# Transposing the normed rows with DMAs instead of TensorE

## The reference, cut to what matters

```python
x = _layernorm(x + _L0_attn_ref(x, ...), axis=-1)

def _L0_ffn_ref(x, wq_gate, s_gate, wq_up, s_up, wq_down, s_down):      # DIM 512, HID 1408
    gate = silu(qlinear(x, wq_gate, s_gate))      # (wq - 128) * scale, summed over DIM
    up = qlinear(x, wq_up, s_up)
    return qlinear(gate * up, wq_down, s_down)

x = _layernorm(x + _L0_ffn_ref(x, ...), axis=-1)
```

## Time and profile before

| | before |
|---|---|
| median of 3 runs | 1080.04 us |
| the profiled execution's own time | 1076.37 us |
| its span, first to last instruction | 1074.6 us |
| PE busy | 1030.4 us (96%) |
| VectorE (DVE) busy | 780.8 us (73%) |
| GpSimd (POOL) busy | 640.9 us (60%) |
| ScalarE (ACT) busy | 465.0 us (43%) |
| mean busy share of the DMA engines, SP's queue | 26.8% |

### The profile page before, as it was taken

One profiled execution on the slowest core, in us unless ns is written; L12 is line 12 of the kernel. 1 busy time (PEld: TensorE's weight loads), 2 busy tenths in 40 slices (PEclk: granted clock), 3 DMA queues, 4 the chain that ended last, 5 costly groups with the idle time before them and its releaser, 6 DMA issues.

```text
span 1074.6 us, 18114 instructions
## 1 busy us (share of the span) xinstructions
PE 1030.4 (96%) x6426; PEld 837.3 (78%) x6426; DVE 780.8 (73%) x1426; ACT 465.0 (43%) x994; POOL 640.9 (60%) x683
## 2 busy tenths in 40 slices
PE   7996889999999999999999999999999999989996
PEld 5576678888888888888888888887878888877774
DVE  6576766787878777786877778786777878676554
ACT  4655443534444344544445343444445344424242
POOL 4456866476756747565764756575674667575210
PEclk9898989999999999999999999999999999999998
DMA  7554302231132222322122222312121211322232
GB/s 231 171 157 152 114 31 59 89 89 50 46 95 77 79 59 80 92 66 70 49 80 88 79 60 87 92 40 89 50 79 50 88 51 42 96 60 79 89 99 79
DMA packets 51640, 89.55 MB, mean 83 GB/s; under 512 B 6298, under 2 KB 11034, under 8 KB 51550
## 3 DMA queue, kind: packets, MB, share of 16 engines
q1 hardware_dynamic: 50786, 88.12, 26.8%
q10 hardware_dynamic: 764, 0.27, 0.1%
HBM read 77.09 MB, written 11.27 MB: 82 GB/s over the span
## 4 chain that ended last, share of the span: by engine, by line
PE 73%; DVE 9%; POOL 7%; issue 7%; ACT 3%; DMA 1%; ACTq 0%; POOLq 0%; DVEq 0%
PE gate_up L997 11%; PE gate_up L998 11%; PE bank L862 9%; PE bank L864 9%; PE bank L863 9%; PE down L1008 6%; PE down L1009 6%; PE bank L958 3%; POOL acc L628 2%; DVE tmp L756 1%; PE bank L980 1%; POOL acc L635 1%; PE spectrum L863 1%; PE spectrum L864 1%; PE spectrum L862 1%
## 5 line engine op out<-in xcount | busy, mean ns | idle before, releaser
L593 ACT ACTIVATE hid<-gate_up,gate_scale 128x256 f32<-128x256 f32 x176 | 83.0, 472 | 208.6 <-PE gate_up L998 204.6
L756 DVE TENSOR_TENSOR tmp<-spectrum,filt 128x512 f32<-128x512 f32 x250 | 169.2, 680 | 0.0
L997 PE MATMUL gate_up<-x2T_hi,wg_sb 128*128 128x256 f16 x704 | 165.8, 276 | 0.0
L634 POOL TENSOR_TENSOR acc<-acc,tmp 128x256 f32<-128x256 f32 x156 | 121.0, 776 | 73.9 <-DVE tmp L756 63.9
L998 PE MATMUL gate_up<-x2T_lo,wg_sb 128*128 128x256 f16 x704 | 163.8, 273 | 0.0
L998 PE MATMUL gate_up<-x2T_lo,wu_sb 128*128 128x256 f16 x704 | 163.3, 273 | 0.0
L997 PE MATMUL gate_up<-x2T_hi,wu_sb 128*128 128x256 f16 x704 | 163.2, 273 | 0.0
L1008 PE MATMUL down<-wd_sb,hid_hi 128*128 128x512 f32 x352 | 148.2, 421 | 5.7 <-DVE tmp L799 3.1
L862 PE MATMUL bank<-xT_hi,win_hi 128*128 128x512 f32 x360 | 150.3, 417 | 2.0 <-POOL win_lo L611 1.7
L864 PE MATMUL bank<-xT_hi,win_lo 128*128 128x512 f32 x360 | 144.3, 401 | 0.0
L863 PE MATMUL bank<-xT_lo,win_hi 128*128 128x512 f32 x360 | 144.3, 401 | 0.0
(11 more groups left out here) (176 smaller groups left out, 2223.4 us busy)
## 6 DMA issues: line engine op xcount, KB each, us to landing
wd_sb<-wd_scratch SPq DMA_DIRECT2D x176, 256.0 KB, 2.6
xstage<-in_x SPq DMA_DIRECT2D x32, 256.0 KB, 4.0
x<-in_x SPq DMA_DIRECT2D x28, 256.0 KB, 2.7
out<-x SPq DMA_DIRECT2D x28, 256.0 KB, 3.2
x<-in_win SPq DMA_DIRECT2D x12, 256.0 KB, 4.8
acc<-in_decay SPq DMA_DIRECT2D x4, 256.0 KB
x<-in_wout SPq DMA_DIRECT2D x4, 256.0 KB, 2.8
x2T_hi<-in_wu SPq DMA_DIRECT2D x4, 256.0 KB, 3.1
```

The costliest lines, as they stand in the source:

```text
L634: G.tensor_tensor(acc[:, i, 0, :], acc[:, i, 0, :], t[:, 1, :], ALU.subtract)
L756: TT(dst, spectrum[j % 2][:, :, :], k_part, ALU.mult).then_inc(made_done, 1)
L997: mm(dst, w[:, kb, rows(q)], x2T_hi[:, kb, ts], start=kb == 0, stop=False)
```

## The change

`x2t` as a step of TensorE is gone, and its use of two banks with it. In beat 0, behind the spectral products of the beat, the list now has `x2split` for both blocks and then one new `x2t` step. ScalarE rounds the normed rows, still in token order, to f16 into a scratch tile (`cv[:, 1, :]` for block 0, `cx1` for block 1, each read as 1024 f16 columns: `hi` in the first 512, `lo` in the others); VectorE writes the rest beside it. The new `x2t` is SP's: four DMAs (`dma_start_transpose`), each of a 128x512 f16 part, write `x2T_hi` and `x2T_lo`, in the order hi of block 0, hi of block 1, lo of block 0, lo of block 1. The first `gu` of a half waits for all four (`x2t_in`). ScalarE's `conv` steps that write the scratch tiles anew wait for them too, and the next half's `x2split`.

```diff
@@ beat_steps, shared
-    if beat == 0 and 0 <= n - 3 < HALVES:
-        steps += [("x2t", n - 3, 0), ("x2t", n - 3, 1)]
...
-    elif beat == 0:
-        steps += spectra[:1] + shared(n, beat) + spectra[1:]
     else:
         steps += shared(n, beat) + spectra
     if beat == 0 and ffn:
-        steps += readers(shared(n, beat))
+        steps += [("x2split", n - 3, 0), ("x2split", n - 3, 1), ("x2t", n - 3)]
@@ scratch
+        def row_parts(b):
+
+            tile = (cv[:, 1, :], cx1[:, :])[b].bitcast(F16)
+            return tile[:, :D], tile[:, D:]
@@ sync
+                elif kind == "x2t":
+                    m, = at
+                    if m == 0:
+                        sp.wait_ge(code_done, NCODE)
+                        for n in range(CODE_SLOTS):
+                            sp.wait_ge(wd_saved[n], 16 * saves_before[n][NCODE])
+                    elif m >= 2:
+                        sp.wait_ge(gate_up_ready, HB * (m - 1))
+                    for part, dst, done in ((0, x2T_hi, x2_hi_done), (1, x2T_lo, x2_lo_done)):
+                        for b in range(2):
+                            sp.wait_ge(done, 2 * m + b + 1)
+                            sp.dma_start_transpose(dst[:, :, rows(pair_block(m, b))], row_parts(b)[part]).then_inc(x2t_in, 16)
@@ scalar
+                    if n >= 3 and (t, c) in ((V, 1), (X1, 0)):
+                        act.wait_ge(x2t_in, 64 * (n - 2))
...
-                    act.wait_ge(bank_ready, k + 1)
...
-                    A(x2T_hi[:, :, rows(pair_block(m, b))], src, ACT.Copy).then_inc(x2_hi_done, 1)
+                    act.wait_ge(ln_done[LN1], 2 * m + b + 1)
...
+                    if m:
+                        act.wait_ge(x2t_in, 64 * m)
+                    A(row_parts(b)[0], row_tile(m, b), ACT.Copy).then_inc(x2_hi_done, 1)
@@ vector
-                    TT(x2T_lo[:, :, ts], src, x2T_hi[:, :, ts], ALU.subtract).then_inc(bank_read, 1)
+                    hi, lo = row_parts(b)
+                    TT(lo, row_tile(m, b), hi, ALU.subtract).then_inc(x2_lo_done, 1)
@@ tensor
-                elif kind == "x2t":
-                    m, b = at
-                    k = use["x2t", m, b]
-                    dst = free_bank(k)
-                    pe.wait_ge(ln_done[LN1], 2 * m + b + 1)
-                    for c in range(CB):
-                        last = nc.tensor.transpose(dst[:, rows(c)], row_tile(m, b)[:, rows(c)], ident[:, :])
-                    last.then_inc(bank_ready, 1)
...
                     if q == 0:
-                        pe.wait_ge(bank_read, use["x2t", m, 1] + 1)
+                        pe.wait_ge(x2t_in, 64 * (m + 1))
```

More of the change, by code:

```diff
@@ L81, in shared @@
     return steps
-READER = {"ip": "conv", "iv": "y", "op": "ln1", "tv": "vsplit", "xt": "xsplit", "x2t": "x2split"}
+READER = {"ip": "conv", "iv": "y", "op": "ln1", "tv": "vsplit", "xt": "xsplit"}
 def readers(products):
@@ L106, in beat_steps @@
         steps += [("norm", LN1, n - 2)]
-    steps += readers([p for p in earlier if p[0] not in ("xt", "x2t")])
+    steps += readers([p for p in earlier if p[0] != "xt"])
     spectra = [("fw", n - 1, j) for j in SPECTRUM_OF_BEAT.get(beat, ())] if convs else []
@@ L212, in build @@
         steps = program()
-        use = count(steps, "xt", "ip", "tv", "iv", "op", "x2t")
+        use = count(steps, "xt", "ip", "tv", "iv", "op")
         convs = count(steps, "conv")
@@ L293, in build @@
         y_step, z_hi_done, z_lo_done = sem("y_step"), sem("z_hi_done"), sem("z_lo_done")
-        res_biased, x2_hi_done = sem("res_biased"), sem("x2_hi_done")
+        res_biased, x2_hi_done, x2_lo_done = sem("res_biased"), sem("x2_hi_done"), sem("x2_lo_done")
+        x2t_in = sem("x2t_in")
         half_down, tail_added, tail_normed = sem("half_down"), sem("tail_added"), sem("tail_normed")
@@ L355, in build @@
         wide_ring = [bank[0][:, :], bank[1][:, :], flat(gate_up[0][:, :, :]), flat(gate_up[1][:, :, :])]
-        wide_uses = use["x2t", 0, 0] // 4 * 4
+        in_shared = ("xt", "ip", "tv", "iv", "op")
+        wide_uses = sum(kind in in_shared for kind, *_ in steps[:steps.index(("x2split", 0, 0))]) // 4 * 4
         def bank_of(k):
@@ L574, in _ @@
                     m, b = at
-                    k = use["x2t", m, b]
-                    act.wait_ge(bank_ready, k + 1)
[L577 to L582, removed]
-                    A(x2T_hi[:, :, rows(pair_block(m, b))], src, ACT.Copy).then_inc(x2_hi_done, 1)
+                    act.wait_ge(ln_done[LN1], 2 * m + b + 1)
+                    n = min(m + 2, HALVES - 1)
+                    if b == 0:
+                        act.wait_ge(bank_ready, use["tv", n, 1] + 1)
+                    else:
+                        act.wait_ge(v1_done, 2 * n + 2)
+                    if m:
+                        act.wait_ge(x2t_in, 64 * m)
+                    A(row_parts(b)[0], row_tile(m, b), ACT.Copy).then_inc(x2_hi_done, 1)
                 elif kind == "silu":
```

## The result

| | before | after |
|---|---|---|
| median | 1080.14 us (10 runs) | 1076.49 us (10 runs) |
| the profiled execution's own time | 1076.37 us | 1074.57 us |
| its span | 1074.6 us | 1072.5 us |

The ratio is 0.9971 (95% interval 0.9961 to 0.9982): 3.1 us faster (1.9 to 4.2). I had said 7.9. The direction is right, the size less than half. The median itself, 1076.49 us, lies at the upper end of the 1069 to 1077 us that I had called likeliest.

The account below looks back on a forecast made before the run. PE was taken to bound the twelve middle stages. Terms -11.2 (middle), -0.2 (m = 0), +3.45 (last three) gave -7.9 us: 1068.5 profiled, 1072.2 as median; likeliest 1069 to 1077, range 1063 to 1092.

Parts of the forecast that it names:

- What goes: PE loses its transpositions in the twelve middle halves: 0.87 us in even, 1.0 in odd halves, 11.2 us gained.
- The latency: From ACT's free time to the last DMA's landing: 0.7 + 3s + landing of 2.3, 6.9 us.
- s: Spacing of the four transposing DMAs' issues on SP: assumed 1.3 us, bounds 0.46 to 2.6.
- rival C: A transposing DMA takes 5.2 us, one after another: latency 21.5 us, some +212 us, 1292 us; chance 0.04.
- rival B: Transpositions go one after another, s and landing 2.6 us: latency 11.1, +45, 1125 us; chance 0.17 with what lies between.
- The cover in the middle: Before PE needs the tiles, 8.2 us (m = 6) and 7.9 (m = 7) hide the latency, 1.0 to 1.3 spare.
- Rival D: Loads of `x` hold the first transposition, or slower subtractions and the tail eat the gain: +1, around 1080 us; chance 0.12.
- The head: At m = 0 the 4.87 us wait for the norm goes, but the norm's new path leaves only 0.2 us gained.
- The tail: In the last three halves cover is short; first `gu` comes 0.7, 1.15 and 1.6 us later, 3.45 us lost.
- Rival A: Transpositions are cheap, spacing 0.46 us, landing 2.0: latency some 4.2 us, all covered, -16.6, 1063.4 us; chance 0.17.

Follow-up runs that it names:

- mid_only: DMAs transpose for halves 1 to 12 only, TensorE as before for 0 and 13 to 15; against the kernel before, ratio 0.9914, 9.3 us faster.
- pair_mid: Two DMAs per half, same bytes, for halves 1 to 12, TensorE for 0 and 13 to 15; against the kernel before, ratio 0.9903, 10.5 us faster.
- the head alone: DMAs transpose for half 0 only, TensorE for the others; against the kernel before, ratio 1.0017, 1.8 us slower.
- second profile: The changed kernel run again with no edit; against the kernel before, ratio 0.9984 (0.9966 to 1.0002), 1.7 us faster.
- the tail alone: DMAs transpose for halves 13 to 15 only, TensorE for the others; against the kernel before, ratio 1.0025, 2.7 us slower.
- head_pe: The changed kernel's four DMAs for halves 1 to 15, half 0 by TensorE; against the kernel before, ratio 0.9967, 3.6 us faster.

## Why the prediction was right or wrong

**What goes, 11.2 us in twelve halves: right in its mechanism, alone 1.9 us too much.** Alone it gave 9.3 us (7.9 to 10.6). The undisturbed stretches show 0.86 and 0.98 us each, as read from the distance between starts. What is missing is, for the most part, the late landings: 1.5 us in the profile of `mid_only`. I had put them at nothing, with one latency for all halves. Two DMAs per half, whose 6.5 us leave over 1 us of cover, get the full gain: -11.7 us in the rows of `pair_mid`.

**The latency, 6.9 us: right in sum, by luck in its main part.** I took s = 1.3 us between ends of 0.46 and 2.6, by halving a load's latency. Measured are 1.27 us held, 1.3 start to start, and a landing of 2.55 (I had 2.3). From ACT's free time to the last landing it is 6.98 to 7.11 us in twelve of the sixteen halves. But the reason for s was wrong: it is not bytes, and halving a load's latency hit 1.3 by chance. 256, 512 and 1024 columns all hold the queue for about 1.2 to 1.34 us. The Trainium skill's 1309 ns for one 128x128 block ("VectorE: DVE Perf Modes", The three transpose paths) lies within the hold of one DMA of two, four or eight blocks, though the section doesn't say what its figure spans, and the landings here take 2.3 us and more; read per block, rival C, it is refuted. The Trainium skill's 350 to 400 GB/s ("Advanced Engine Details and Errata", X-Bar Transpose (TRN2)) are not reached at these sizes: 256 KB each 1.34 us is 196 GB/s, and the changed kernel's DMAs move half that. One sum of rival B is off: at s = 1.7 my terms give -2.1 us, not -2.8; the sign still turns near 1.75.

**The cover in the middle: right.** 8.2 and 7.9 us against 7.0, and no wait in ten halves of twelve (0.33 us at m = 12, 0.07 at m = 5). Eight DMAs, with 12 us, went through the cover in each half. Rival D is refuted for its place: at m = 7 the first transposition, behind the loads of `x`, lands 4.3 us after issue, the last one 2.56, with PE full.

**The head, -0.2 us: wrong, this is the step whose mechanism failed.** The prediction had "0.2 us gained, not 4.87", from the same latency after the same norm. So it came: the first gate product stands 7.15 us after the norm, against 7.13. But I took that for the end of the account, and put what the clock does behind the new wait at nothing.

What filled the 7.13 us before was not the path of the tile. The second subtraction had written `x2T_lo` at 141.13, 4.4 us ahead of the gate product. From 137.83 to 145.52 PE never waited; it worked off the transpositions and the two beats behind them, and 4.27 us of that work ran at half clock (granted 0.50). The rows of before: the first matmul behind the transpositions (they take 1.59 us from start to start, 0.79 at m = 6), the window of half clock, which begins in the wait for the norm, and the one from the transpositions to the gate product:

```profile
139.42 0.56 PE L862 MATMUL spectrum<-vT_hi,fwd_hi 128*128 128x256 f32 x1
```

```profile
135.30:142.10 6.80, 4.27 (x17) 4.04 (x18) 2.59 (x6) 3.57 (x6) 3.30 (x4) 0.50 0.11 42
137.83:145.52 7.69, 7.69 (x38) 7.00 (x39) 4.97 (x8) 3.41 (x7) 3.96 (x7) 0.72 0.00 1
```

So the old 7.13 us held PE's own work, with its loss to the half clock, and when the gate products began the clock was full again. In the changed kernel PE does those two beats earlier, where it used to sit idle. It then idles 5.88 us up to the landing, and the half clock falls on the gate products behind. PE's rows at the four longest waits of the changed kernel (the first is m = 0, then 13, 14, 15):

```profile
147.07 0.40 PE L1001 MATMUL gate_up<-x2T_hi,wg_sb 128*128 128x256 f16 x1 [5.88 <-DMA x2T_lo<-cx]
939.52 0.28 PE L1001 MATMUL gate_up<-x2T_hi,wg_sb 128*128 128x256 f16 x1 [2.77 <-DMA x2T_lo<-cx]
990.19 0.28 PE L1001 MATMUL gate_up<-x2T_hi,wg_sb 128*128 128x256 f16 x1 [1.29 <-DMA x2T_lo<-cx]
1030.15 0.28 PE L1001 MATMUL gate_up<-x2T_hi,wg_sb 128*128 128x256 f16 x1 [2.67 <-DMA x2T_lo<-cx]
```

The windows behind the first two of them, in the changed kernel, and then the one from the first gate product of m = 0 before:

```profile
147.07:151.20 4.13, 4.13 (x18) 3.10 (x19) 1.68 (x3) 0.99 (x3) 1.34 (x2) 0.50 0.60 187
939.70:943.10 3.40, 3.40 (x19) 2.53 (x17) 3.06 (x6) 0.12 (x1) 2.23 (x4) 0.51 0.30 105
```

```profile
145.52:149.60 4.08, 4.08 (x28) 3.36 (x28) 3.75 (x7) 2.65 (x5) 3.39 (x5) 1.00 0.00 0
```

18 matmuls at clock 0.50 (1.2 GHz) against 28 at 1.00 (2.4 GHz) in the same time: 4.1 us at half clock lose 2.1. Less up to 0.8 where TensorE's way took 7.9 to the first gate product, that is 1.3 to 2.1; the head alone measured +1.8 us (0.9 to 2.8). The term was -0.2 and is +1.8.

The same sum can be done from PE's idle time. The work at half clock is as long in both kernels (4.27 and 4.2 us). But PE idles 0.31, 1.19 and 5.88 us between the first forward transform of beat 0 and the gate product, 7.4 us where it idled 4.87, and saves only 0.8 us of transposing: +1.7. Work that moves from behind a wait to before it makes the wait longer.

**The tail, +3.45 us: right alone, half again as much in the whole kernel.** Alone it measured +2.7 us (1.4 to 3.9), an interval that contains my 3.45. In the changed kernel the three stretches lose 5.6 us, in the second profile of it 5.5. The difference is at m = 13: there the wait is 2.77 us (2.62 in the second profile) where the tail alone has 1.47, because the last DMA lands 3.97 us after its issue instead of 2.55; and the 3.4 us that follow run at clock 0.51 with 19 matmuls (window above), while behind the shorter wait the same place of the tail-only kernel has

```profile
949.90:953.30 3.40, 3.40 (x30) 3.19 (x31) 3.33 (x8) 0.89 (x2) 3.19 (x5) 1.00 0.41 150
```

30. The late landing costs 1.3 us, and the clock could account for the 1.3 us that the stretch to m = 14 is longer. All three profiles with a wait of 2.6 to 3.0 us at m = 13 (the changed kernel twice, `head_pe`) have the half clock behind it and a stretch of 50.7 us to m = 14, the tail-only kernel with 1.47 us has neither (49.4). I read this from rows and ran nothing that separates landing and clock.

**Sum.** Measured one by one: -9.3 + 1.8 + 2.7 = -4.8 us. The whole measured -3.1 (1.9 to 4.2) and -1.7 (-0.2 to 3.7). The intervals are too wide to prove a rest. The changed kernel's own rows, from the first gate product of m = 0 on, do close: -11.1 in the middle (the eleven stretches, and 1.0 us of work that is gone from the stretch to m = 1), +1.8 for the head (that stretch is 0.9 us longer instead of 1.0 shorter), +5.6 in the tail, which makes -3.6. Against my terms that is nothing in the middle, 2.0 us at the head, and 2.2 in the tail, by the late landing at m = 13 and what follows it. Late landings I had put at nothing; here they cost at m = 13, in `mid_only` in the middle.

Rival A, which I gave 0.17, is refuted: s is 1.3 us. The two-DMA version gets its full gain in the middle, because there are fewer DMAs and not because s is small, but its 10.6 us in all are not A's 16.6.

## What to carry to other kernels

A transposing DMA had a price per instruction here: 1.2 to 1.34 us of its queue, whatever it moved between 256 and 1024 columns, and 2.4 to 3.3 us from issue to landing. So make them few and wide (from four to two per half was worth 7 to 9 us), and count the queue's part of the latency in issues, not in bytes. Where the bound engine reaches a step as early as before, ask still what it did meanwhile: here it had worked, and now it waits, and the work behind the wait ran at half clock. That happened behind the waits of 2.6 to 5.9 us at m = 0, at m = 13 and at all twelve places of the eight-DMA version, and not behind the 2.7 us at m = 15. Where a term is a margin (8 us of cover, 7 of latency), look for what is late now and then, since it pays at each of its places.

## What was not expected of the hardware

- The hold of the queue: 1.25 us for a 128x256 transposition, 1.20 to 1.27 for 128x512, 1.24 to 1.34 for 128x1024; landing 2.4, 2.55, 3.3 us after issue.
- Landings are late where an instruction fetch is in flight. In the changed kernel's record of DMA packets the queue called q8 in the page moves pieces of 16384 bytes, 50 in the run, that take 0.9 to 1.4 us each, where a transposition's 544 packets (512 of 256 bytes, 32 of 4) take at most 0.02 each in the median. The three halves whose last transposition landed over 3.4 us after issue (m = 5, 12, 13: 3.49, 4.15, 3.97) all have one in flight at that time (450.66, 877.16, 936.68), and in the second profile it is the same halves (3.38, 4.12, 3.82), again with one in flight. The edits of the other kernels moved the fetches, and the late landings moved with them: in `mid_only` and `head_pe` they are at m = 4 and 11 instead of 5. Over all six profiles with four DMAs per half, all 13 last transpositions with a fetch in flight within 2.55 us of their issue landed after 3.38 to 4.25 us, and the 50 without one after 3.07 at most. With two DMAs per half it is not so clean: ten last landings took over 3.5 us, and only three of them had a fetch in flight in their first 3.3 us. The link is inferred from the times; nothing was run for the purpose of moving a fetch.
- A weight load issued right behind the transpositions holds SP for 0.58 us (in 15 of 16 halves of the changed kernel; 1.5 at m = 13) instead of 0.32 to 0.43.
- The first 140 us of the same program differ by up to 5.7 us between executions (the norm of m = 0 ends at 136.99 to 142.67), the rest by tenths. Two profiles of this kernel are compared stretch by stretch, not end to end.
